# An adaLN/FFN kernel on one core: x's first chunk moves to SyncE's queue, the small vectors to ScalarE's

## The reference, cut to what matters

```
x  = x + moe(cond0(x, ids_8))     # x: 8 batches x 256 tokens x 128
x  = x + ffn(cond1(x, ids_4))

cond0: relu(x @ wi.T + 2*common_lora + 2*expert_lora[id of the batch]) and the same form back to 128
moe:   4 rounds:  logits = cur @ Wg[r] + bg[r];  two best of 4 experts, softmax weights cw
                  cur += sum_e cw[e] * (gelu(cur @ W1[e] + b1[e]) @ W2[e] + b2[e])
cond1: low-rank product with lora_A[id], lora_B[id], plus lang_embed[id]
ffn:   silu(h @ w1*s1) * (h @ w2*s2), two gelu layers 512 x 512, one layer back to 128
```

## Time and profile before

| what | value |
|---|---|
| device time, median of 3 runs | 481.57 us |
| the three runs | 480.96, 481.77, 481.57 us |
| the profiled execution | 480.82 us |
| its span, first to last instruction | 479.0 us |
| TensorE busy | 474.5 us, 99% of the span |
| VectorE, ScalarE, GpSimd busy | 388.0, 393.6, 121.7 us |
| granted TensorE clock, mean | 1.000 |

### The profile page before, as it was taken

One profiled execution on the slowest core, in us unless ns is written; L12 is line 12 of the kernel. 1 busy time (PEld: TensorE's weight loads), 2 busy tenths in 40 slices (PEclk: granted clock), 3 DMA queues, 4 the chain that ended last, 5 costly groups with the idle time before them and its releaser, 6 DMA issues.

```text
span 479.0 us, 7437 instructions
## 1 busy us (share of the span) xinstructions
PE 474.5 (99%) x2260; PEld 395.0 (82%) x2260; DVE 388.0 (81%) x638; ACT 393.6 (82%) x543; POOL 121.7 (25%) x102
## 2 busy tenths in 40 slices
PE   9999999999999999999999999999999999999997
PEld 8998888888888888888888888888888888888886
DVE  5898999999989898988889898889897758654343
ACT  4889888888889898888888798898888888697643
POOL 4995212121211212122212121171313144500000
PEclk9999999999999999999999999999999999999999
DMA  8603702021120202020202112120202000000001
GB/s 236 191 24 134 285 0 91 2 88 42 48 88 0 88 0 88 0 88 0 88 1 88 45 43 88 44 90 0 88 2 88 2 0 0 1 1 0 0 23 69
DMA packets 8299, 27.03 MB, mean 56 GB/s; under 512 B 2258, under 2 KB 3602, under 8 KB 6098
## 3 DMA queue, kind: packets, MB, share of 16 engines
q1 hardware_dynamic: 7090, 22.45, 13.4%
q0 software_dynamic: 288, 2.88, 1.7%
q10 hardware_dynamic: 896, 1.38, 1.0%
HBM read 25.26 MB, written 1.44 MB: 56 GB/s over the span
## 4 chain that ended last, share of the span: by engine, by line
PE 96%; POOL 2%; DMA 1%; DVE 0%; SPq 0%; issue 0%; ACT 0%; DVEq 0%
PE bank L538 34%; PE bank L541 34%; PE bank L544 26%; POOL ffn_lo L442 1%; PE bank L638 1%; PE bank L639 1%; DMA stage<-lora_all 1%; PE bank L565 0%; PE bank L562 0%; POOL xlo L447 0%; DVE stage L1076 0%; DVE prod L1076 0%; ACT ffn_hi L842 0%; DVE x L1312 0%; SPq L251 0%
## 5 line engine op out<-in xcount | busy, mean ns | idle before, releaser
L859 ACT ACTIVATE act_out<-bank,vec 128x512 f32<-128x512 f32 x256 | 164.9, 681 | 40.5 <-PE bank L544 28.7
L1154 DVE TENSOR_TENSOR hid_lo<-act_out,hid_hi 128x1024 fp32r<-128x1024 f32 x128 | 158.5, 1258 | 31.6 <-ACT hid_hi L864 31.5
L864 ACT ACTIVATE hid_hi<-act_out 128x1024 fp32r<-128x1024 f32 x128 | 135.9, 1062 | 8.3 <-ACT act_out L859 0.4
L502 POOL TENSOR_TENSOR cur<-cur,prod 128x512 f32<-128x512 f32 x48 | 64.8, 1350 | 233.5 <-DVE prod L1165 233.1
L538 PE MATMUL bank<-hid_hi,moe_hi 128*128 128x512 f32 x256 | 99.8, 390 | 0.0
L544 PE MATMUL bank<-hid_hi,moe_lo 128*128 128x512 f32 x256 | 99.7, 390 | 0.0
L541 PE MATMUL bank<-hid_lo,moe_hi 128*128 128x512 f32 x256 | 99.7, 389 | 0.0
L538 PE MATMUL bank<-xhi,moe_hi 128*128 128x512 f32 x256 | 99.6, 389 | 0.0
L541 PE MATMUL bank<-xlo,moe_hi 128*128 128x512 f32 x256 | 99.6, 389 | 0.0
L544 PE MATMUL bank<-xhi,moe_lo 128*128 128x512 f32 x256 | 99.6, 389 | 0.0
L538 PEld LDWEIGHTS bank<-hid_hi,moe_hi 128*128 128x128 f32 x256 | 48.1, 188 | 11.1
(11 more groups left out here) (134 smaller groups left out, 570.6 us busy)
## 6 DMA issues: line engine op xcount, KB each, us to landing
cw_all<-cw_dram SPq DMA_DIRECT2D x16, 1024.0 KB, 4.7
stage<-ffn_w POOLq DMA_DIRECT2D x1, 2304.0 KB, 8.5
cw_all<-moe_w SPq DMA_DIRECT2D x4, 512.0 KB, 7.5
stage<-lora_all SPq DMA_DIRECT2D x5, 160.0 KB, 4.6
x<-x_t SPq DMA_DIRECT2D x3, 256.0 KB, 5.2
out_t<-x SPq DMA_DIRECT2D x3, 256.0 KB, 2.4
cur<-cond_base ACTq DMA_DIRECT2D x2, 256.0 KB, 3.4
stage<-ffn_w POOLq DMA_DIRECT2D x1, 512.0 KB, 3.9
```

The lines of the kernel that those rows point to most:

```text
L502: pool.tensor_tensor(cur[:, c, :], cur[:, c, :], prod[:, s % 2, :], ALU.add).then_inc(add_done, 1)
L859: act.activation(act_out[:, f // 2, f % 2, :], bank[:, f, :], ACT.Gelu_apprx_tanh, bias=vec[:, V_B1 + e * FC + f:V_B1 + e * FC + f + 1]).t ...
L864: act.activation(hid_hi[:, s % 2, 2 * pr:2 * pr + 2, :], act_out[:, pr, :, :], ACT.Copy)\
L1154: dve.tensor_tensor(hid_lo[:, s % 2, 2 * pr:2 * pr + 2, :], act_out[:, pr, :, :], hid_hi[:, s % 2, 2 * pr:2 * pr + 2, :].bitcast(F32), ALU ...
```

## The change

Two lines go from SyncE's stream and one comes in; in ScalarE's stream one goes and the same two come in. SyncE's stream becomes: `ids`, x's chunk 0, the wait for `ids`, the factor loads. ScalarE's becomes: `base` part 0, `vec`, `gbias`, the table load, the 1x1 activation, the wait for `ids`, the factor loads. No other instruction, semaphore or wait is touched.

```diff
         def _(sp):
             sp.dma_start(ids[:], batch_ids).then_inc(ids_in, 16)
-            sp.dma_start(vec[:], vecs).then_inc(small_in, 16)
-            sp.dma_start(gbias[:], gate_bias.to_broadcast([SQ, ROUNDS * EXPERTS])).then_inc(small_in, 16)
+            x_load(sp, 0)
             sp.wait_ge(ids_in, 16)
...
             base_load(act, 0)
-            x_load(act, 0)
+            act.dma_start(vec[:], vecs).then_inc(small_in, 16)
+            act.dma_start(gbias[:], gate_bias.to_broadcast([SQ, ROUNDS * EXPERTS])).then_inc(small_in, 16)
             act.wait_ge(const_done, 1)
```

## The result

The changed kernel is **slower**: 482.66 us (median of 16 runs, 481.45 to 483.29) against 481.14 us of the kernel before (median of 16 runs, 480.59 to 482.16), a ratio of 1.0028 with a 95% interval of 1.0022 to 1.0035. In microseconds that is 1.3 (by the ratio) to 1.5 (by the medians). The forecast was +0.05 us, between -0.09 and +0.25, and no measurable difference. The profiled execution took 481.97 us, its span is 480.1 us.

What follows compares the result with a forecast made beforehand. TensorE's steady work from 18.04 us was taken as the bound, movable only through merge group 0's start. SyncE's 0.09 us gain and ScalarE's 0.2 us delay mostly cancel: +0.05 us, 481.6 us on the 481.57 median, range 480.9 to 482.1.

Steps and rivals of the forecast that it cites:

- read the id on time rather than early: SyncE's opening: id read near 2.04 us, gaining 0.09; the early case, read at 1.74, gaining 0.39, had chance 0.10.
- split_gate stayed covered: Opening, gbias on ScalarE's queue: landing near 4.6 us, with 0.4 us of cover, 0.8 with the slack behind x0_low.
- x's chunk 0 with nothing to spare: Opening: x0_low would end at 6.98 us at worst, just covered before the first sum at 6.99.
- What else each moved instruction touches: Side effects, all costed at nothing; first item: base part 1 out 0.1 to 0.39 us later, about 0.9 us of cover.
- none of these loads is in the chain: SyncE's queue behind the factors: batch 2, x's chunks 1 to 3 and later weights go out 0.09 us earlier, costing nothing.
- "after 9.5": Sign at VectorE's third sum: the forecast is wrong if base part 1 arrives after 9.5 us; no chance given.
- GpSimd's gap: Sign on GpSimd: the forecast is wrong if it has a gap between 8.4 and 16 us; no chance given.
- the four rivals: At the opening: ids early (0.10), factors behind x (0.08), slower by the clock (0.04), nothing else, the forecast (0.78).
- Rival 3: First merges: a later start drops TensorE to 1.2 GHz, +1.2 us on the merges, 482.8 us or more; chance 0.04.
- rival 2: SyncE's queue: batch 0's factors behind x's 256 KB take 3.4 us, landing at 6.12, +0.4 us, 482.0; chance 0.08.
- the place in a queue shows no price here: Factor loads: median 2.8 us by either queue, behind 512 KB or 29 KB, so splitting base and x gains nothing.

Runs made afterwards that it cites:

- e13: Changed kernel plus a useless 2 KB load on SyncE's queue between the factors of batches 0 and 2: 481.06 us, ratio 1.0002 to the kernel before.
- e6: Kernel before with x's chunk 1 issued ahead of batch 2's factors on SyncE's queue: 482.55 us, ratio 1.0032.
- e5: Changed kernel with no sum waiting for base part 1 (every sum adds base part 0): 481.23 us, ratio 1.0006 to the kernel before.
- e4: The changed kernel run again, unaltered: 482.30 us, ratio 1.0023 to the kernel before.
- e10: Kernel before with no sum waiting for base part 1 (every sum adds base part 0): 480.98 us, ratio 0.9999.
- e11: Changed kernel plus one 2 KB load on SyncE's queue behind the moe weights, restoring its old number of DMAs: 482.95 us, ratio 1.0029 to the kernel before.
- e2: Changed kernel with x's chunk 1 issued by SyncE behind batch 4's factors: 482.13 us, ratio 1.0019 to the kernel before.
- e7: Changed kernel with x's chunk 1 held on SyncE's queue until batch 1's factors landed: 482.01 us, ratio 1.0022 to the kernel before.
- e1: Changed kernel with gbias alone back on SyncE's queue, behind x's chunk 0: 481.09 us, ratio 1.0002 to the kernel before.
- e3: Kernel before plus one unused 2 KB load on ScalarE's queue just ahead of base part 1: 482.81 us, ratio 1.0040.
- e8: Kernel before with base part 1 issued by ScalarE ahead of batch 3's factors: 481.94 us, ratio 1.0020.
- e9: Kernel before with x's chunk 1 held on SyncE's queue until batch 1's factors landed: 480.94 us, ratio 0.9996.
- e12: Kernel before with base part 1 loaded as two halves, one by ScalarE's queue, one by SyncE's: 481.10 us, ratio 1.0002.

## Why the prediction was wrong

**What held.** The first 18 us set the end. SyncE read the id on time rather than early: its factors went out at 2.69 us, 0.12 earlier, and not 0.39. ScalarE's went out at 2.92, 0.25 later (0.2 forecast). The two cancelled at merge group 0 and a little more: it started at 5.62, not 5.75, since the factors took 2.5 to 2.6 us from issue and not 2.8 to 2.9. split_gate stayed covered, and x's chunk 0 with nothing to spare: the first sum, at 6.84, waited for neither base nor small vectors, but VectorE came to it from x0_low without a gap, where it had idled 0.40 us before it. TensorE lost nothing to its clock. The two issue times were right within 0.05 us, and the landing that counted, that of batch 1's factors, within 0.15 us; batch 0's came some 0.3 us earlier than forecast. T1 moved by -0.15 us. That is no gain shown: T1 lies anywhere between 6.72 and 7.63 us in the seven profiles that keep the opening of the kernel before.

**The step that failed** is the first item under "What else each moved instruction touches": base part 1, costed at nothing. It has two errors, and by the prediction's own numbers either alone would have cost 0.1 us at most.

- *The slip.* The prediction let base part 1 land as much later as it is issued, 0.1 to 0.39 us. It was issued 0.23 us later and landed 1.0 us later. Its duration from issue to landing was taken as fixed. The trace of the kernel before already spoke against that: the same 160 KB load takes 3.4 us on one queue and 4.0 on the other in the same stretch, and four loads of 160 and 256 KB are issued within 0.8 us while the shared DMA engines are nearly full (busy share 0.95 at 267 GB/s from 5 to 10 us, and still 0.97 at 16 us). At that rate 256 KB take about 1.0 us and 160 KB about 0.6 (an estimate), so a load that gets ahead can cost far more than the 0.2 us by which it does. The leads between them were 0.14 and 0.17 us, less than the delay forecast for ScalarE. The prediction moved SyncE's queue earlier and ScalarE's later in separate paragraphs and never put the two lists of times side by side; there the order of both pairs flips (e13, e6). SyncE's later loads, issued 0.09 us earlier and set aside because "none of these loads is in the chain", are the other half of the same step.
- *The cover.* 0.9 us was read from GpSimd's need for the third weight at 10.92. But VectorE's third sum has a second user, the sums behind it. From 8.62 to 12.3 us VectorE sums without a gap, and TensorE's next merges need the last of these sums. They start at 12.49, and at 13.36 after, where the trace shows them waiting for it. The cover is what the two paths leave between them: T3 may be 1.98 us behind T1, and was 8.62 - 6.99 = 1.63. That is 0.35 us, not 0.9. To find it one has to follow everything that is queued behind the late instruction on its own engine, and not only the tile's next reader.

The changed kernel's median loss, 1.3 to 1.5 us, is then: base part 1's wait, about 1.1 us by e5 against the changed kernel (0.8 against e4); the rest of some 0.3 us lies between e5 and e10 (1.0006 and 0.9999, whose intervals overlap), and a longer end is its likely place, which is not shown. The two profiles differ by 1.1 us: 0.67 at VectorE's last operation and 0.43 in the issue of the last store. ScalarE's last store issue took 0.78 us in the changed kernel's profile, 0.68 in e4, 0.64 in e11 and 0.43 to 0.49 in the four others that keep ScalarE's changed opening (e2, e5, e7, e13), against 0.35 to 0.37 in seven profiles with the old opening or e1's (before, e1, e3, e6, e8, e9, e12), and 0.74 in an eighth (e10). What makes it is open; the number of SyncE's DMAs isn't it (e11).

The prediction's list of signs did contain this one, base part 1 "after 9.5", and GpSimd's gap. It was given no chance of its own: the four rivals all looked at merge group 0, and the side on which the loss came, slower by more than 0.2%, had 0.05. Rival 3, the only one to reach it but for the tail of rival 2, was the wrong mechanism. The absolute forecast of 481.6 us stood on the median of three runs, 481.57; the 16 runs put the kernel before at 481.14. So 481.6 missed by 1.1 us where the forecast shift of +0.05 missed by 1.3 to 1.5, and the smaller miss is luck.

The Trainium skill (DMA: Bandwidth & Descriptors, section Issuing engines are not separate DMA queues) says that loads from different engines run on the same DMA engines and interleave, and that issuing from several saves only the sequencer's time, usually small beside the transfer. The prediction took it as agreeing with its own reading that "the place in a queue shows no price here". The traces fit the shared engines: what one engine issues changes when the other's loads land (e6, e13). The issue time is small beside the transfer here too, 0.23 against 4.8 us, but it was not a small term: it decided 1.0 us of the landing.

## What to carry to other kernels

When an edit shifts one issuing engine against another, write all large loads of both in one list by time of issue, before and after, and look for pairs that change places; where the DMA engines are full, such a pair can cost far more than the shift (here 1.0 us at the landing for 0.23 us at the issue), and a small extra load on the other engine can undo it. The cover of a late tile is the least over all that is queued behind its first user on that engine, not the slack of the next reader. And where an edit moves the critical path by only a tenth of a microsecond, ask which second path lies within a few tenths: here it was 0.35 us behind.

## What the runs showed of the hardware

- The landing of a 256 KB load in a full stretch scatters strongly between executions: issued at 4.82 or 4.83 us behind the same loads, it took 4.8, 5.2, 5.5 and 6.4 us (changed kernel, e4, e5, e11). Issued at 4.59 or 4.60 in the kernel before, e1 and e10 it took 4.0, 4.8 and 4.1. One profile is no measure of it; medians of the device time tell more.
- The moment at which TensorE comes up to speed scatters too, in kernels whose opening is alike, and it enters T1. The same first merges of e7 and of the changed kernel, whose warm-up started at the same 1.06 us:

```profile
5.78 1.22 PE L562 MATMUL bank<-stage 32*128 32x512 f32 x2
...
7.70 1.16 PE L634 MATMUL bank<-blank 128*128 128x128 f32 x8
```

```profile
5.62 0.70 PE L561 MATMUL bank<-stage 32*128 32x512 f32 x2 [0.38 <-DMA stage<-lora_all]
...
7.09 1.16 PE L633 MATMUL bank<-blank 128*128 128x128 f32 x8
```

  1.22 us against 0.70 for the same two merges, and T1 is 7.70 against 6.84, though the merges of e7 waited for no factors. The warm-up matmul took 275 ns from 4.7 us on in the changed kernel, and still 421 ns in e7 up to its end. The granted clock reads 1.00 for this stretch in both, so only the durations show it. Between these two executions it makes nearly 0.9 us of T1; e3 (1.22 us, T1 7.63) and e5 (0.99 us, T1 7.25) were late in the same way.
